# Attention kernel on one core: three on-chip sums moved from VectorE and GpSimd to accumulating DMAs, with four product slots

## The reference

```
q, v = layernorm(x), ctx                    # k = v = ctx
corr = ifft(fft(q) * conj(fft(v))).real     # over the 512 rows, per channel
w, idx = top_k(corr, 12); w = softmax(w)
out[p] = sum_i w_i * v[min(idx_i + p, 511)]
x = x + out
```

## Time and profile before

| | |
|---|---|
| median of 3 runs | 2239.98 us (2239.89 to 2240.15) |
| span of the profiled execution | 2240.4 us |
| busy in the span: PE, POOL, DVE, ACT | 2170.8, 1570.1, 1712.2, 1222.0 us |
| attention steps | up to about 1404 us |
| feed-forward tiles | from there to the end |

### The profile page before, as it was taken

The page is one execution under the profiler, slowest core; times in us unless marked ns, Lnnn a source line. Parts: engine busy times, 40 slices in busy tenths (PEclk is TensorE's granted clock), DMA queues, the critical chain, the costliest instruction groups (busy, mean ns, idle before and its releaser), DMA issues.

```text
span 2240.4 us, 30428 instructions
## 1 busy us (share of the span) xinstructions
PE 2170.8 (97%) x9664; PEld 1460.5 (65%) x9664; DVE 1712.2 (76%) x4081; ACT 1222.0 (55%) x2486; POOL 1570.1 (70%) x1023
## 2 busy tenths in 40 slices
PE   4899999999999999999999998899999999999999
PEld 2466565565565565565565564687888888787887
DVE  7999999999999999999999999744544444454443
ACT  4576676676676676676655535544434334443431
POOL 6899999999999999999999987433333333333420
PEclk9999999999999999999999999999999999999999
DMA  8132332332332332332321245544444444444431
GB/s 288 65 120 99 111 110 99 116 106 99 118 104 99 118 104 99 118 103 99 103 82 61 91 164 176 186 157 164 151 162 166 167 160 161 157 159 161 164 116 57
DMA packets 110420, 287.84 MB, mean 128 GB/s; under 512 B 7136, under 2 KB 7264, under 8 KB 109152
## 3 DMA queue, kind: packets, MB, share of 16 engines
q1 hardware_dynamic: 110304, 286.45, 37.1%
HBM read 219.32 MB, written 67.11 MB: 128 GB/s over the span
## 4 chain that ended last, share of the span: by engine, by line
PE 77%; DVE 11%; POOL 5%; issue 4%; ACT 2%; DMA 1%; SPq 0%; DVEq 0%; POOLq 0%; ACTq 0%
PE pair L691 7%; PE out L528 5%; PE out L530 5%; PE out L529 5%; PE z L528 5%; PE z L530 5%; PE z L529 5%; PE evac L602 4%; PE evac L603 4%; PE pair L528 4%; PE evac L578 4%; PE pair L530 4%; PE pair L529 4%; PE lag L642 4%; PE pair L591 4%
## 5 line engine op out<-in xcount | busy, mean ns | idle before, releaser
L1549 POOL TENSOR_TENSOR rows<-rows,cin 128x1024 f32<-128x1024 f32 x48 | 117.9, 2456 | 355.8 <-DMA rows<-out_dram 292.8
L691 PE MATMUL pair<-r_f,back 128*128 128x512 f32 x768 | 335.4, 593 | 0.0
L1495 POOL TENSOR_TENSOR r_f<-prod 128x1024 f32<-128x1024 f32 x128 | 306.0, 2402 | 24.0 <-DVE prod L931 22.1
L691 PEld LDWEIGHTS pair<-r_f,back 128*128 128x128 f32 x768 | 143.3, 190 | 167.8 <-issue 167.8
L528 PE MATMUL pair<-w_hi,wts_hi 128*128 128x512 f32 x512 | 206.5, 403 | 4.9 <-DVE w_lo L1049 2.9
L1244 ACT ACTIVATE xt_full<-tp 128x512 f32<-128x512 f32 x128 | 74.8, 584 | 245.4 <-PE tp L547 242.0
L528 PE MATMUL out<-b_hi,zt_hi 128*128 128x512 f32 x512 | 205.8, 402 | 1.5 <-ACT zt_hi L1433 1.5
L528 PE MATMUL z<-a_hi,xt 128*128 128x512 f32 x512 | 203.0, 397 | 1.9 <-DVE xt L888 1.9
L530 PE MATMUL pair<-w_hi,wts_lo 128*128 128x512 f32 x512 | 200.5, 392 | 0.0
L529 PE MATMUL pair<-w_lo,wts_hi 128*128 128x512 f32 x512 | 200.4, 391 | 0.0
L529 PE MATMUL z<-a_lo,xt 128*128 128x512 f32 x512 | 200.1, 391 | 0.0
(11 more groups left out here) (193 smaller groups left out, 5619.2 us busy)
## 6 DMA issues: line engine op xcount, KB each, us to landing
out_dram<-att_sb SPq DMA_DIRECT2D x32, 1024.0 KB, 4.3
rows<-out_dram SPq DMA_DIRECT2D x64, 512.0 KB, 3.6
cin<-out_dram SPq DMA_DIRECT2D x64, 512.0 KB, 4.0
xin<-in_x_dram SPq DMA_DIRECT2D x64, 512.0 KB, 3.7
out_dram<-rows SPq DMA_DIRECT2D x64, 512.0 KB, 2.6
vf<-in_ctx_dram SPq DMA_DIRECT2D x31, 1024.0 KB, 5.2
xf<-in_x_dram SPq DMA_DIRECT2D x30, 1024.0 KB, 5.1
stat_in<-in_x_dram SPq DMA_DIRECT2D x28, 1024.0 KB, 5.1
```

Of the source, the lines that this page charges most:

```text
L691: return nc.tensor.matmul(pair_ps[:, bank, :], back[:, 3 * bank + n, :], r_f[:, row, :], start=n == 0, stop=n == 2)
L1495: nc.gpsimd.tensor_tensor(dst, prod[:, slot, 0:2, :], prod[:, slot, 2:4, :], ALU.add).then_inc(add_done, 1)
L1549: nc.gpsimd.tensor_tensor(half, first, second, op).then_inc(c_added, 1)
```

## The change

`prod` becomes four slots of two blocks. DVE now writes the cosine product straight into its destination (`p_f` or `r_f`) and the sine product into a slot. What was "slot half + slot half" becomes "destination + slot":

- both x sums and weights' sums 1 and 3 stay POOL adds of the same size, in place;
- weights' sums 0 and 2 are accumulating DMAs of 512 KB from the slot into `r_f`, issued by POOL (`send_products`, semaphores `neg_summed` and `cyc_summed`).

The last sum of the output halves leaves DVE (except in the last step). ACT copies the even part as before and then the odd part (`copy_odd`, at the end of the step, straight behind `copy_even`); in the next step, after the two negations, it writes the even part a second time and the negated odd part (`double_halves`); POOL then issues one accumulating DMA of 1 MB into `att_sb` (`sum_halves`), between the first half of the x fold and `fold_w` of tiles 2 and 3. SP stores `att_sb` one step later than before, after the `stat_in` load. The constant row (L1386) waits for the DMA of sum 2, the first output rows for the DMA of sum 0, and `copy_even` for the later store.

```diff
-        prod = sb("prod", [P, 2, 4, CH])
+        prod = sb("prod", [P, 4, 2, CH])
...
+                if i > 1 and not is_step(i, GROUPS):
+                    store_summed(k, r, i - 1)
...
+            def store_summed(k, r, g):
+                sp.wait_ge(att_summed, 16 * g)
+                sp.dma_start(at_group(att_t, k, r, -2), att_sb[:]).then_inc(stored, 16)
...
                     pe.wait_ge(prod_ready, prod_w(i, 2) + 1)
-                    pe.wait_ge(add_done, prod_w(i, 1) + 1)
+                    pe.wait_ge(neg_summed, 16 * i)
+                    pe.wait_ge(add_done, add_w(i, 1) + 1)
...
-                    pe.wait_ge(add_done, prod_w(i, 2) + 1)
+                    pe.wait_ge(cyc_summed, 16 * i)
                     pe.wait_ge(dc_put, i)
...
-                def products(idx, pair, vs, plus_one):
+                def products(first, pair, second, vs, plus_one):
...
-                    if not (isinstance(idx, int) and idx < 2):
-                        dve.wait_ge(add_done, idx - 1)
...
-                    nc.vector.tensor_tensor(slot[:, 2:4, :], s_ps, vs[:, 1:3, :], ALU.mult).then_inc(prod_ready, 1)
+                    nc.vector.tensor_tensor(second, s_ps, vs[:, 1:3, :], ALU.mult).then_inc(prod_ready, 1)
...
+                        elif not is_step(i, 1):
+                            dve.wait_ge(att_summed, 16 * (i - 1))
+                        products(r_f[:, 2 * blk:2 * blk + 2, :], n % 2, prod[:, n, :, :], vs, blk < 2)
...
-                if b:
+                if is_step(i, GROUPS):
                     dve.wait_ge(even_copied, i)
                     dve.wait_ge(pair_ready, pair_out(i, 1) + 1)
...
-                    nc.scalar.activation(att_sb[:, 2:4, :], pair_ps[:, 0:2, :], ACT.Copy).then_inc(even_copied, 1)
+                    nc.scalar.activation(att_sb[:, 0:2, :], pair_ps[:, 0:2, :], ACT.Copy).then_inc(even_copied, 1)
+
+                def copy_odd():
+                    act.wait_ge(pair_ready, pair_out(i, 1) + 1)
+                    nc.scalar.activation(prod[:, 2, :, :], pair_ps[:, 2:4, :], ACT.Copy).then_inc(att_done, 1)
+
+                def double_halves(g):
+
+                    act.wait_ge(even_copied, g)
+                    nc.scalar.activation(att_sb[:, 2:4, :], att_sb[:, 0:2, :], ACT.Copy).then_inc(att_doubled, 1)
+                    act.wait_ge(att_done, g)
+                    nc.scalar.activation(prod[:, 3, :, :], prod[:, 2, :, :], ACT.Copy, scale=-1.0).then_inc(att_doubled, 1)
...
+                if i > 1:
+                    double_halves(i - 1)
...
-                    act.wait_ge(add_done, prod_w(i, 2) + 1)
+                    act.wait_ge(cyc_summed, 16 * i)
...
                     copy_even()
+                    if a:
+                        copy_odd()
...
+            def send_products(idx, slot, dst, signal):
+                pool.wait_ge(prod_ready, idx + 1)
+                nc.gpsimd.dma_start(dst, prod[:, slot, :, :], accum_op=ALU.add).then_inc(signal, 16)
+
             def add_products(idx, slot, dst):
                 pool.wait_ge(prod_ready, idx + 1)
-                nc.gpsimd.tensor_tensor(dst, prod[:, slot, 0:2, :], prod[:, slot, 2:4, :], ALU.add).then_inc(add_done, 1)
+                nc.gpsimd.tensor_tensor(dst, dst, prod[:, slot, :, :], ALU.add).then_inc(add_done, 1)
+
+            def sum_halves(g):
+
+                pool.wait_ge(att_doubled, 2 * g)
+                nc.gpsimd.dma_start(att_sb[:], prod[:, 2:4, :, :].rearrange("p n s c -> p (n s) c"),
+                                    accum_op=ALU.add).then_inc(att_summed, 16)
...
+                if i > 1:
+                    sum_halves(i - 1)
                 if b:
                     for t in (2, 3):
                         fold_w(i - 1, t)
...
-                        add_products(prod_w(i, n), n % 2, r_f[:, 2 * blk:2 * blk + 2, :])
+                        if n % 2:
+                            add_products(prod_w(i, n), n, r_f[:, 2 * blk:2 * blk + 2, :])
+                        else:
+                            send_products(prod_w(i, n), n, r_f[:, 2 * blk:2 * blk + 2, :], (neg_summed, cyc_summed)[n // 2])
```

More of the change, by code:

```diff
@@ L234, in build_program @@
         even_copied, att_done, stored = sem("even_copied"), sem("att_done"), sem("stored")
+        att_doubled, att_summed = sem("att_doubled"), sem("att_summed")
+        neg_summed, cyc_summed = sem("neg_summed"), sem("cyc_summed")
         rows_loaded = [[sem(f"rows_loaded{n}_{h}") for h in range(2)] for n in range(RING)]
@@ L305, in prod_w, with add_x, add_w @@
             return 6 * i - 2 + n - (2 if is_step(i, GROUPS) else 0)
+        def add_x(i, n):
+            return n if is_step(i, 0) else 4 * i - 2 + n
+        def add_w(i, n):
+            return 4 * i + n // 2 - (2 if is_step(i, GROUPS) else 0)
         def corr_at(i, t, second):
@@ L1029, in body @@
                         dve.wait_ge(minus_done, 4 * i + n + 1)
-                        products(prod_x(i, n), n, v_cyc[cur][:, 3 * n:3 * n + 3, :], False)
+                        if not is_step(i, 0):
+                            dve.wait_ge(lag_ready, CT * i)
+                            if is_step(i, 1):
+                                dve.wait_ge(add_done, add_x(0, n) + 1)
+                            elif n == 0:
+                                dve.wait_ge(neg_summed, 16 * (i - 1))
+                            else:
+                                dve.wait_ge(add_done, add_w(i - 1, 1) + 1)
+                        products(p_f[:, 2 * n:2 * n + 2, :], n, prod[:, n, :, :], v_cyc[cur][:, 3 * n:3 * n + 3, :], False)
                         if n == 0 and not (is_step(i, 0) or is_step(i, 1)):
@@ L1065, in body @@
                         vs = (v_cyc if blk < 2 else v_neg)[before][:, 3 * (blk % 2):3 * (blk % 2) + 3, :]
-                        products(prod_w(i, n), n % 2, vs, blk < 2)
+                        if n == 0 and not is_step(i, 1):
+                            dve.wait_ge(pair_ready, pair_out(i - 1, 1) + 1)
+                        if n < 2:
+                            if a:
+                                dve.wait_ge(add_done, add_x(i, n) + 1)
+                            elif n == 0:
+                                dve.wait_ge(neg_summed, 16 * (i - 1))
+                            else:
+                                dve.wait_ge(add_done, add_w(i - 1, 1) + 1)
+                        elif not is_step(i, 1):
+                            dve.wait_ge(att_summed, 16 * (i - 1))
+                        products(r_f[:, 2 * blk:2 * blk + 2, :], n % 2, prod[:, n, :, :], vs, blk < 2)
                         if n == 0 and s and r == 3:
@@ L1557, in _ @@
             pool.wait_ge(v_loaded, 16)
-            first = prod[:, 1, :, :]
+            first = prod[:, 2:4, :, :].rearrange("p n s c -> p (n s) c")
             nc.gpsimd.tensor_tensor(first[:, 0:2, :], vf[:, 0:4:2, :], vf[:, 1:4:2, :], ALU.add)
@@ L1585, in body @@
                 if a:
-                    if not is_step(i, 0):
-                        pool.wait_ge(lag_ready, CT * i)
                     for n in range(2):
```

26 lines of the change are left out of this document (12 added, 14 removed).

## The result

The changed kernel takes 2399.86 us (median of 4 runs, 2398.84 to 2404.69), the kernel before 2240.07 us in the same comparison: ratio 1.071, 95% interval 1.070 to 1.073. That is slower by 160 us, where 75 us were forecast (2315 us). The range, 2261 to 2425, holds the result. The direction and the chain of waits were right; the size was not, because one term of the sum, sum 2's landing, was taken far too early. The profiled execution spans 2397.0 us, 156.6 us more than before.

What follows compares the result with a forecast made beforehand. PE leads the chain of waits (77%), with DVE and POOL almost full. Terms: 30 x (0.9 + 0.3 + 1.5) = 81 us, less 6.7, on 2240.4 gives 2314.7, forecast 2315 us; range 2261 to 2425.

Steps and rivals of the forecast that it cites:

- sum 2's landing: DMA of weights' sum 2, awaited by ACT's constant row: lands at 597.0, 1.5 us past the slack in each of 30 steps.
- The loop of the turn and ACT's queue: Step-closing loop: PE weights' spectra, DVE fourth product and top-12, ACT's run to L1271, PE; exponentials and copies queue behind L1386.
- The slack: At ACT's constant row: sum 2 may land until 595.46 without anybody late; 1.68 us of slack at tile 0's exponentials.
- slow rival: Accumulation far slower than a copy: sum 2 lands 5.2 us past the slack, +185 us, 2426 us; chance 23%.
- `copy_odd`: ACT copy between `copy_even` and L1271 at the turn: nothing covers it, +0.9 us a step from 30 turns.
- `double_halves`: Two ACT copies, 2.0 to 2.3 us together, in place of the 2.05 us wait DVE's relief opens: 0.
- POOL's issue: Time for POOL to issue a DMA: taken as 1.0 us, between 0.38 and 2.4 us.
- The 0.3 us behind it: POOL's fold starts 0.3 us late after `sum_halves`, delaying x sums and PE's L642: +0.3 us a step.
- Sum 0 covered: DMA of weights' sum 0 lands at 590.9 before PE's output rows at 591.53: covered by 0.6 us.
- `att_summed` and the later store: The 1 MB accumulation and the output store, due before DVE's third product and `copy_even`: both covered at 0.
- The 6.7 us: Gain in 6 long steps, 1.1 us each, from taking the output sums off DVE.
- The last steps: A store now stands between SP's loads for the first tiles: 0 to some us, left in the range.

Runs made afterwards that it cites:

- w_dma_only: Changed kernel with only the weights' sums 0 and 2 as accumulating DMAs; output halves summed by DVE and stored early, as before the change: 2303.7 us.
- sp_behind: Changed kernel, but SP issues the `stat_in` load and the output halves' store only after sum 2 of the same step has landed: 2329.1 us.
- sum2_only: w_dma_only with weights' sum 0 put back on POOL as an in-place add, leaving sum 2 alone as a DMA: 2291.4 us.
- slots_odd: slots_only plus one unused ACT copy of 1024 columns straight behind `copy_even`: 2241.6 us.
- att_no_double: Changed kernel with all weights' sums as POOL adds and without the two doubling copies on ACT, so output halves are not formed: 2247.5 us.
- sum0_only: w_dma_only with weights' sum 2 put back on POOL as an in-place add, leaving sum 0 alone as a DMA: 2234.6 us.
- slots_only: Changed kernel without accumulating DMAs: four slots and products in place kept, weights' sums on POOL, output halves summed by DVE, stored as before: 2235.0 us.
- after_fed: Changed kernel with zero-matrix matmuls added on PE during its two waits at the turn: 2397.4 us.

## Why the prediction was half the size

Point by point, in its own order.

**The loop of the turn and ACT's queue** were right. The slack was right too. From the constant row to `copy_even` ACT's list takes 7.0 us where the row is late (mean of w_dma_only and of after), against 10.1 before, so the row could start 10.1 - 7.0 = 3.1 us later than 2.8 us behind the product: 5.9 us. The prediction had a landing at 595.46 for a product at 589.67, 5.8 us.

**Sum 2's landing was the step that failed.** The prediction had 1.0 for the issue, 5.1 for the transfer and 1.2 for company: 7.3 us behind the product. Undisturbed it is about 5 us (sp_behind), so the first two together were too long by 1 us. Beside the `stat_in` load it is 7.7 to 7.9 us (sum2_only, w_dma_only), beside load and store 10.1 us. Company costs 5 us and not 1.2, and past the slack are 10.1 - 5.9 = 4.2 us a step and not 1.5. The prediction took a quarter of one transfer though it had two in the same microsecond; its slow rival, with 5.2 us, was nearer. The DMA issues of the changed kernel show the sizes with medians over the run:

```profile
r_f<-prod POOLq DMA_DIRECT2D x64, 512.0 KB, 5.1
out_dram<-att_sb SPq DMA_DIRECT2D x32, 1024.0 KB, 11.2
...
att_sb<-prod POOLq DMA_DIRECT2D x31, 1024.0 KB, 8.4
```

The first median also holds sum 0, which has no such company and takes 4.6 us (median of its 32), and so hides sum 2. The section "Issuing engines are not separate DMA queues" of "DMA: Bandwidth & Descriptors" in the Trainium skill, which the prediction weighed, says that transfers run on the same 16 DMA engines and interleave, whichever engine issued them. The runs agree: 5.0, 7.8 and 10.1 us with none, one and two transfers beside it. The Trainium skill's fit for a DMA from GpSimd, in the section "Anatomy of one DMA — SWDGE (gpsimd) path" of the same page, gives an estimate of 3.2 us for 512 KB; the shortest accumulation measured here took 4.5 us.

**How often.** The prediction multiplied by 30. It costs much only where `stat_in` is loaded, in 22 whole steps and the first; an interval without that load grew by 0.6 us. The rows had the count of 28 loads, four of them ahead of the first `copy_even`.

**`copy_odd`**, 0.9 us a step: 0.26 measured (slots_odd).

**`double_halves`**, 0: 0.51 us a step measured (att_no_double). Its cover, DVE's part that ends sooner, did not hide all of it.

**POOL's issue**, 1.0 us estimated: 0.88 measured, and 0.90 for the halves. The 0.3 us behind it wasn't isolated. The wait of PE for the second `p_f` sum, 0.2 us before, is 0.4 us once in the stretch 560 to 850.

**Sum 0 covered:** right (sum0_only). `att_summed` and the later store are covered in the changed kernel as forecast: the store issued at 652.60 takes about 11 us and `copy_even` starts at 669.42.

**The 6.7 us** of the long steps were right in size (slots_only: 6.6 us) and had the wrong cause. DVE still makes the output sums in slots_only, so it isn't their removal; the four slots, or the products written in place, give it, for which the prediction had 0. In the stretch 500 to 850 us before, DVE's cosine product waited 5.9 us in 7 waits, up to 1.3 us, for POOL's add in `r_f`; in slots_only DVE has no wait for POOL there. That this is the whole reason was not tested.

**The last steps**, left at 0 to some us, cost 19.2 us. The chain of waits there, from the trace of the changed kernel:

```profile
1459.44 6.96 DMA att_sb<-prod
...
1468.46 7.10 DMA cin<-out_dram
1475.69 2.41 POOL rows L1608
1478.24 2.40 POOL rows L1611
...
1483.50 10.86 DMA r_f<-prod
```

SP's store waits for the halves' transfer, and the loads for the first feed-forward tiles stand behind it in SP's list. POOL adds what they bring (L1608, L1611) ahead of its last sums in its own list, and so issues sum 2 some 3 us late, among those loads. No run tests this part by itself.

**PE's clock** was in no term: about 1 us a step (after_fed).

The terms with what was measured, for a step with a `stat_in` load: sum 2 past its slack 4.2 us; from `copy_even` to the next third product 28.3 - 26.6 = 1.7 us, in which are `copy_odd`, the doubling copies and the clock; together 5.9, against 6.0 for the difference of the intervals. How the 1.7 us divide inside the changed kernel was only shown for each alone (0.26, 0.51, about 1), and they needn't add.

## What to carry to other kernels

An accumulating DMA is free where its first reader comes late, and expensive where another engine's list has unrelated work behind that reader: cost it by what is queued there, and move that work ahead of the wait first (64 of 69 us here). Before putting a DMA on a path, list what every other queue issues just before or within its flight, and add a price for each; here it was 2 to 3 us for every 1 MB. Ask of each such transfer what holds it back to that moment, for a wait further up in the same list can bring several at once. Then multiply by the steps that have that company. A change of several parts is worth splitting: here the part that needed no DMA was the gain.

## What the chip showed that I had not expected

- From the start of its issue to its landing a 512 KB accumulation from SBUF to SBUF took 4.5 us at the least. Beside one load of 1 MB it took 7.7 us in the mean (6.2 to 9.5, 23 steps of w_dma_only), beside a load and a store of 1 MB each 9.7 us (9.1 to 10.5, 23 steps of the changed kernel). In most of these steps the load was issued 0.9 us and the store 0.5 us ahead of it. One of 1 MB took 8.4 us (median of 31). The issue itself occupied POOL for 0.88 us.
- After a wait of 3.0 us, with one of 1.7 us some 7 us before it, the granted clock of PE was 0.82, 0.50 and 0.83 in three windows of 2 us one behind the other, 0.50 being the 1.2 GHz level. It was 1.00 in the windows on both sides of them.
